# A causal softmax layer of a four-layer kernel: the order of the first transfers, and unread products on TensorE in the head

## The chip, the cores and the metric

The kernel runs on one core of a Trainium2 chip. The metric is the time of one execution on the device, in microseconds (us). Several executions are made, and their median is given.

## The reference

Four blocks are applied one after another to x of shape (8, 1024, 256), each as x + layernorm(block(layernorm(x))): causal softmax attention with 16 heads of 16, a linear layer, linear attention with a small feed-forward part, and a mixture of eight experts. The change touches only the part of the kernel that computes the first two, and there the softmax attention:

```python
qkv = x @ W_qkv + b_qkv
q, k, v = jnp.split(qkv, 3, axis=-1)          # 16 heads of 16
att = jnp.einsum('bhqd,bhkd->bhqk', q, k) * SCALE
att = jnp.where(causal, att, -jnp.inf)
att = jax.nn.softmax(att, axis=-1)
y = jnp.einsum('bhqk,bhkd->bhqd', att, v)
return y.transpose(0, 2, 1, 3).reshape(B, T, C) @ W_proj + b_proj
```

## The kernel before

`softmax_layer` works through the eight batches, one a turn. Five instruction streams (SyncE, TensorE, ScalarE, GpSimd, VectorE) are written out by hand and meet only at semaphores. Each stream has a part `before()`, the head, which prepares batch 0, and then `turn(b, ...)` for each batch.

**A turn** has 48 steps k: four head groups of four heads, twelve segments (`SEGS`) each. In a step TensorE does two pairs of score products (`scores`, K by Q, 50 rows of the array, two heads in the two halves of the array at once), two pairs of products for the row maxima (`maxima`, Q by K, 48 rows) of the segment 16 steps later (LM = 16), and the value products (`values`) of step k - 2. VectorE reduces the maxima products (`reduce`), with a mask added where a tile lies on the diagonal. ScalarE takes the exponentials of the scores. Maxima and scores share a ring R of three slots in PSUM, `psum_r`.

**Units** are further pieces of TensorE work, one after certain k by the table `UNIT_AT`, in a ring G of one slot, `psum_g`. Head units prepare the next batch: T1 (transposes of the normed x), QK (six products of 128x128x512 that make a half of Q or K for eight heads, in split precision), V. Tail units (END, YT, P, T2, F) finish the batch before. OUT and N belong to the batch itself: OUT transposes the attended values, and N transposes the maxima, which VectorE negates and splits (`minus`) and SyncE puts into `q_st` (`minus_max`, four transfers); the scores of the head group wait for them. Turn 0 has no tail units (`with_tail` is false). With them absent, steps 0 to 7, 9 and 10 of turn 0 have no unit but N 1 at 8; steps 28 to 31 have none either. `G.wait_free(pe, r, u)` waits until the unit before u has been evacuated.

**The head** runs T1, QK 0 to 3 and V 0 to 3. ScalarE copies each QK product to `parts` with its bias, GpSimd splits it in two. `stack(0, hg)` on SyncE then moves Q and K of head group hg from `parts` into `q_st` and `k_st` in twelve transfers of 128 KB; the head's first group waits for the splits of QK 0 to 3. TensorE's maxima of mk = 0 wait for all of stack(0, 0), those of mk = 12 for stack(0, 1). Maxima for mk = 0 to 15 follow, with QK 4 to 7 after mk = 4 to 7 and N 0 after mk = 12. Before ScalarE writes QK 4 into `parts` it waits for both stacks, which read that tile:

```python
if i % 4 == 0 and b + m > 0:
    for hg in (2 - 2 * m, 3 - 2 * m):
        act.wait_ge(stacked[hg], (b + m) * STACK)
```

`load_x(1, 0, GU_BEFORE)` is the load of batch 1 into `x_in`, 1 MB. It waits until the last T1 unit of batch 0 has been evacuated. VectorE first reads it at k = 1 of turn 0. All of SyncE's transfers are issued in program order, each after its own waits.

Of the kernel before, what the change touches and what calls it, by code (L numbers as in the profile page):

```python
# [15 lines left out]
P = 128  # L16
B, T, D = 8, 1024, 256
N = B * T
# [3 lines left out]
HALF = 512  # L22
# [100 lines left out]
def of_batch(view, b):  # L123
    return view[bass.ds(b, 1), :, :, :].rearrange("a p j d -> p (a j) d")
# [170 lines left out]
def softmax_layer(nc, ctx, ident, minus_half, spot, x_rows, W_qkv, b_qkv, W_proj, b_proj, weight,  # L295
# [13 lines left out]
    NSEG = len(SEGS)  # L309
# [7 lines left out]
    def sb(name, shape, dt=F32):  # L317
        return ctx.enter_context(nc.sbuf_tensor(name, shape, dt))
# [6 lines left out]
    psum_g = ctx.enter_context(nc.psum_tensor("a_general", [P, HALF], F32))  # L325
# [6 lines left out]
    w_qkv = {part: sb(f"w_qkv_{part}", [P, CD, 3 * D], F32R) for part in ("hi", "lo")}  # L332
# [167 lines left out]
    def kept(what, with_head, with_tail):  # L500
        if what[0] in TAIL_UNITS:
            return with_tail
        return with_head or not (what[0] in HEAD_UNITS or what == ("N", 4))
# [5 lines left out]
    def r_units(u0, with_head):  # L509
        units = {}  # L510
        for k in range(NK):
            for pair in range(2):
# [5 lines left out]
    H_SEQ = ([("T1", i) for i in range(4)] + [("QK", i) for i in range(4)] +  # L518
             [("V", i) for i in range(4)] + [("QK", i) for i in range(4, 8)] + [("N", 0)])
# [4 lines left out]
    GU_BEFORE = {what: i for i, what in enumerate(H_SEQ)}  # L524
# [8 lines left out]
    G = Ring(sem, "a_general", 1, PER_G)  # L533
# [40 lines left out]
    def of_sync(sp, prepare):  # L574
# [11 lines left out]
        def load_x(b, r, U):  # L586

            G.wait_evacuated(sp, r, U["T1", 3])
            sp.dma_start(x_in[:, :, :], of_batch(xv, b)).then_inc(x_loaded, 16)

        def stack(b, hg, used=None):

            if used is not None:
                sp.wait_ge(pv_done, used + PV0)
            if hg % 2 == 0:
                sp.wait_ge(split_done, 8 * b + 4 * (hg // 2) + 4)
            for qk, terms, st in ((0, QPART, q_st), (1, KPART, k_st)):
                for t, part in enumerate(terms):
                    for h2 in range(2):
                        to = 64 * h2 + DH0 * t  # L600
                        src = 64 * (hg % 2) + 32 * h2
                        sp.dma_start(
                            st[to:to + DH0, 2 * hg:2 * hg + 2, :].bitcast(F32),
                            parts[src:src + 32, qk, part, :].bitcast(F32)
                            ).then_inc(stacked[hg], 16)
# [22 lines left out]
        def turn(b, U, with_head, with_tail, more, prepare=None):  # L628
# [21 lines left out]
                sp.wait_ge(x2_stored, b * 16)  # L650
            sp.dma_start(x_res[:, :, :], of_batch(xv, b)).then_inc(res_loaded, 16)

        load_x(1, 0, GU_BEFORE)
        stack(0, 0)
        stack(0, 1)
        minus_max(0, 0, GU_BEFORE, 0)
        stack(0, 2)
# [22 lines left out]
    def of_tensor(pe, prepare):  # L680
        def four_turned(src, of, c):
            for j in range(4):
                last = nc.tensor.transpose(psum_g[:, j * P:(j + 1) * P], of(src, j, c),
                                           ident[:, :])
            return last

        def tile_of(half):
            return lambda src, j, c: src[:, half * 4 + j, c * P:(c + 1) * P]
# [10 lines left out]
        def two_tiles_split(i, lhs, rhs):  # L699
            for jj in range(2):  # L700
                j = 2 * i + jj
                terms = [(c, a, w) for c in range(CD) for a, w in PRODUCTS]
                for t, (c, a, w) in enumerate(terms):
                    last = nc.tensor.matmul(psum_g[:, jj * D:(jj + 1) * D],
                                            lhs[a][:, c, j * P:(j + 1) * P], rhs[w][:, c, :],
                                            start=(t == 0), stop=(t == len(terms) - 1))
            return last

        def unit(b, r, U, what):


            name, i = what
            u = U[what]
            if name == "T1":
                pe.wait_ge(head_norm, b * 4 + 2 * (i // CD) + 2)
            elif name == "T2":
                pe.wait_ge(tail_norm, b * 4 + 2 * (i // CD) + 2)
            elif name in ("OUT", "END"):
                v = i if name == "OUT" else 2 * HG - 1
                pe.wait_ge(attended, b * 2 * HG + v + 2)  # L720
            elif name == "N":
                pe.wait_ge(mx_ready, b * HG + i % HG + 1)
            G.wait_free(pe, r, u)
            if name == "T1":
                last = four_turned(x_in, tile_of(i // CD), i % CD)
            elif name == "T2":
                last = four_turned(att, tile_of(i // CD), i % CD)
            elif name == "YT":
                last = four_turned(y, tile_of(i // CD), i % CD)
            elif name in ("OUT", "END"):  # L730
                half = v % 2
                last = four_turned(oT, lambda src, j, c: src[:, half, j * P:(j + 1) * P], 0)
            elif name == "N":
                par = i % 2
                last = nc.tensor.matmul(psum_g[0:32, 0:P],
                                        mx[:, par, :, :, :].rearrange("p h r j -> p (h r j)"),
                                        ident[:, :], start=True, stop=True)
            elif name == "QK":
                m, qk, half = i // 4, i // 2 % 2, i % 2
                terms = [(c, a, x) for c in range(CD) for a, x in PRODUCTS]  # L740
                for t, (c, a, x) in enumerate(terms):
                    last = nc.tensor.matmul(psum_g[:, :],
                                            w_qkv[a][:, c, qk * D + m * P:qk * D + (m + 1) * P],
                                            xnT[x][:, c, half * HALF:(half + 1) * HALF],
                                            start=(t == 0), stop=(t == len(terms) - 1))
            elif name == "V":
                last = two_tiles_split(i, xnT, {part: w_qkv[part][:, :, 2 * D:3 * D] for part in w_qkv})
            elif name == "P":
                last = two_tiles(i, yT, w_proj)
            elif name == "F":  # L750
                last = two_tiles(i, yT, w_ffn)
            last.then_inc(G.full[0], 1)

        def maxima(b, r, U, mk, pair):
            hg, (j, k0, k1) = mk // NSEG % HG, PIECES[mk % NSEG]
            u, w = U["M", mk, pair], k1 - k0
            if mk % NSEG == 0 and pair == 0:
                pe.wait_ge(stacked[hg], (b + 1) * STACK)
            R.wait_free(pe, r, u)
            for h2 in range(2):  # L760
                rows = slice(64 * h2, 64 * h2 + KQ)
                last = nc.tensor.matmul(psum_r[:, R.slot(u), h2, 0:w],  # L762
                                        q_st[rows, 2 * hg + pair, j * P:(j + 1) * P],
                                        k_st[rows, 2 * hg + pair, k0:k1], start=True,
                                        stop=True)
            last.then_inc(R.full[R.slot(u)], 1)
# [35 lines left out]
        def batch_of(b, what):  # L802
            if what[0] in TAIL_UNITS:
                return b - 1
            return b + 1 if what[0] in HEAD_UNITS or what == ("N", 4) else b

        def turn(b, U, RU, with_head, with_tail, prepare=None):
            for k in range(NK):
                more = k + LM < NK or with_head
                scores(b, RU, k, 0)  # L810
                if more:
                    maxima(b + (k + LM) // NK, b, RU, k + LM, 0)
                if k > 1:
                    values(b, RU, k - 2)
                elif with_tail:
                    values(b - 1, RU_TURN, NK - 2 + k)
                scores(b, RU, k, 1)
                if more:
                    maxima(b + (k + LM) // NK, b, RU, k + LM, 1)
                if k in UNIT_AT and kept(UNIT_AT[k], with_head, with_tail):  # L820
                    unit(batch_of(b, UNIT_AT[k]), b, U, UNIT_AT[k])

        def before():
            for what in H_SEQ[0:12]:
                unit(0, 0, GU_BEFORE, what)
            for mk in range(LM):
                for pair in range(2):
                    maxima(0, 0, RU_BEFORE, mk, pair)
                if 4 <= mk < 8:
                    unit(0, 0, GU_BEFORE, ("QK", mk))  # L830
                if mk == NSEG:
                    unit(0, 0, GU_BEFORE, ("N", 0))

        turns(turn, before, prepare)

        def last_values():
# [2106 lines left out]
```

## Time and profile before

| what | value |
|---|---|
| median of three runs | 4213.46 us (4207.55 to 4227.06) |
| the profiled execution, its own time | 4220.28 us |
| its span | 4218.5 us |
| its mean granted TensorE clock | 0.963 |
| TensorE busy | 3896.9 us, 92% of the span |
| VectorE busy | 2709.6 us, 64% |
| head of the softmax layer | 0 to 103.6 us, where k = 0 of turn 0 begins |
| k = 0 to 15 | 103.6 to 165.5 us in turn 0, 261.5 to 315.7 us in turn 1 |

Times in the rows count from the start of the span. In a row of windows stand the window, its length, then the busy us (and instructions begun) of PE (TensorE's products), PEld (its weight loads), DVE (VectorE), ACT (ScalarE) and POOL (GpSimd), then the granted clock, the busy share of the 16 transfer engines, and GB/s. In a row of waits stand who waited for whom, us in total, times, and the longest. In a timeline, a row is the start, the length until the last of the merged instructions ended, the engine, the line of the kernel, the operation with what it writes and reads, and in brackets the idle time before it and what ended it. The granted clock is a share of the full 2.4 GHz: 1.00 is 2.4 GHz, 0.50 is 1.2 GHz, and a value between the two is a stretch with some of each.

### The profile page before, as it was taken

Reading aid. Unit: us, or ns where it says so; the run is one execution under the profiler, and the core shown is the slowest. Engines: PE = TensorE matmul, PEld = TensorE weight load, DVE = VectorE, ACT = ScalarE, POOL = GpSimd, SP = SyncE. Lnnn points to the kernel's source line nnn. Section 1 sums busy time; section 2 is a strip of 40 time slices with the busy share of each in tenths; the row PEclk is TensorE's granted clock in tenths of the full one; section 3 lists DMA queues with packets and bytes.
Section 4 is the critical chain, followed back from the end, with each engine's and each line's share of the span. In section 5 each row is a group of like instructions: output and inputs, shape, how many; then the busy total and the mean of one; then the engine's idle time right before and its main releaser. Section 6 shows DMA issues by size and latency. Waiting matters only on the chain. (4 is left out here: it accounts for less than half of the span.)

```text
span 4218.5 us, 74666 instructions
## 1 busy us (share of the span) xinstructions
PE 3896.9 (92%) x28676; PEld 3028.7 (72%) x28676; DVE 2709.6 (64%) x7827; ACT 2115.5 (50%) x3994; POOL 1162.1 (28%) x1097
## 2 busy tenths in 40 slices
PE   4999999999999899999999999999999699999992
PEld 2444444444445788888888888888888599999992
DVE  5788988888885566555565665555565555555555
ACT  1566666666666555555455554454454333333323
POOL 3234344343332211111112111111111133333334
PEclk8799999999988999999999999999999799999996
DMA  3543543544441100000000000000001133333336
GB/s 70 98 87 50 114 92 57 97 92 67 77 100 53 36 26 21 21 21 23 18 22 22 22 20 17 16 20 11 18 20 34 52 65 71 70 65 69 70 60 191
DMA packets 176195, 227.06 MB, mean 54 GB/s; under 512 B 27276, under 2 KB 152299, under 8 KB 175840
## 3 DMA queue, kind: packets, MB, share of 16 engines
q1 hardware_dynamic: 147808, 185.86, 19.3%
q0 software_dynamic: 26736, 31.70, 4.9%
q8 instruction: 228, 3.74, 0.4%
q10 hardware_dynamic: 1296, 4.72, 0.3%
q14 instruction: 127, 1.04, 0.1%
HBM read 90.63 MB, written 87.05 MB: 42 GB/s over the span
## 5 line engine op out<-in xcount | busy, mean ns | idle before, releaser
L882 ACT ACTIVATE probs<-a_scores 128x1024 f32<-128x1024 f32 (+3 forms) x768 | 615.5, 811 | 342.7 <-PE a_scores L776 337.3
L1036 DVE CUSTOM_DVE_ANT_0 a_scores<-a_scores,mask 128x384 f32<-128x384 f32 (+3 forms) x1024 | 480.3, 513 | 107.9 <-PE a_scores L762 102.4
L776 PEld LDWEIGHTS a_scores<-q_st,k_st 50*128 50x128 f32 x1536 | 149.6, 192 | 358.9 <-issue 206.6
L275 POOL TENSOR_TENSOR l_ln_rstd<-l_ln_ve,minus_half 128x4 f32<-128x4 f32 x80 | 81.9, 1023 | 1047.2 <-DVE l_ln_ve L248 1046.8
L1844 ACT ACTIVATE l_o<-l_num,l_den 128x64 f32<-128x64 f32 x960 | 222.0, 319 | 291.4 <-DVE l_den L2330 286.6
L776 PE MATMUL a_scores<-q_st,k_st 50*128 50x512 f32 (+3 forms) x1536 | 350.6, 454 | 11.6 <-DVE mx L1036 5.4
L762 PE MATMUL a_scores<-k_st,q_st 48*128 48x512 f32 (+3 forms) x1536 | 307.6, 398 | 50.6 <-ACT probs L882 23.0
L796 PE MATMUL a_out<-probs,v_aug 128*32 128x512 f32 (+3 forms) x3072 | 348.6, 528 | 3.5 <-POOL probs L963 3.3
L1039 DVE TENSOR_REDUCE mx<-a_scores 128x2 f32<-128x1024 f32 x256 | 309.8, 1221 | 59.3 <-PE a_scores L762 58.3
L963 POOL TENSOR_SCALAR_AFFINE_SELECT probs<-probs 128x512 f32<-128x512 f32 x256 | 164.2, 642 | 524.0 <-ACT probs L882 515.0
L2647 PE MATMUL e_out<-e_weights_hi,e_hT_hi 128*128 128x256 f32 x1088 | 303.8, 279 | 0.0
L2647 PE MATMUL e_out<-e_weights_hi,e_hT_lo 128*128 128x256 f32 x1088 | 303.8, 279 | 0.0
L2647 PE MATMUL e_out<-e_weights_lo,e_hT_hi 128*128 128x256 f32 x1088 | 303.7, 279 | 0.0
L2694 ACT ACTIVATE e_to_split<-e_hidden,e_b 128x384 f32<-128x384 f32 (+1 forms) x320 | 200.0, 625 | 196.9 <-PE e_hidden L2632 196.5
L1753 PE MATMUL l_num<-l_v,l_scores_kept 128*128 128x65 f32 x2048 | 285.1, 262 | 0.0
L1753 PEld LDWEIGHTS l_num<-l_v,l_scores_kept 128*128 128x128 f32 x2048 | 270.0, 192 | 0.0
L1858 ACT ACTIVATE l_o<-l_general 128x512 f32<-128x512 f32 x256 | 152.6, 596 | 219.4 <-PE l_general L1602 200.3
L2716 POOL DMA_INDIRECT expert_sums_scratch<-e_y,e_number x136 | 222.6, 1637 | 69.7 <-issue 37.4
L762 PEld LDWEIGHTS a_scores<-k_st,q_st 48*128 48x128 f32 x1536 | 155.0, 198 | 115.0 <-ACT probs L882 80.2
L2231 DVE TENSOR_TENSOR l_a<-l_general,l_a 128x512 f32<-128x512 f32 x64 | 44.3, 692 | 299.2 <-PE l_general L1561 160.8
L2632 PE MATMUL e_hidden<-e_rT_hi,e_weights_hi 128*128 128x384 f32 (+1 forms) x640 | 233.8, 365 | 0.0
L1748 PE MATMUL l_num<-l_state,l_qT 128*128 128x130 f32 x1024 | 231.0, 307 | 0.0
(278 smaller groups left out, 10560.3 us busy)
## 6 DMA issues: line engine op xcount, KB each, us to landing
q_st<-parts SPq DMA_DIRECT2D x192, 128.0 KB, 4.5
k_st<-parts SPq DMA_DIRECT2D x192, 128.0 KB, 6.8
expert_rows_scratch<-empty_row SPq DMA_DIRECT2D x34, 520.0 KB, 9.6
l_x<-x_scratch SPq DMA_DIRECT2D x32, 512.0 KB, 3.8
e_weights<-in_L_ffn_W_dram SPq DMA_DIRECT2D x16, 1024.0 KB, 6.9
e_rows<-expert_rows_scratch SPq DMA_DIRECT2D x24, 390.0 KB, 3.2
e_rows<-expert_rows_scratch SPq DMA_DIRECT2D x16, 520.0 KB, 3.8
x_in<-in_L_attn_x_dram SPq DMA_DIRECT2D x8, 1024.0 KB, 5.5
```

What stands on the lines that cost most here:

```text
L762: last = nc.tensor.matmul(psum_r[:, R.slot(u), h2, 0:w], q_st[rows, 2 * hg + pair, j * P:(j + 1) * P], k_st[rows, 2 * hg + pair, k0:k1], s ...
L776: last = nc.tensor.matmul(psum_r[:, R.slot(u), h2, 0:w], k_st[rows, 2 * hg + pair, i * P:(i + 1) * P], q_st[rows, 2 * hg + pair, q0:q0 + w ...
L796: last = nc.tensor.matmul(psum_o[32 * h4:32 * h4 + 32, q0 - half * HALF:HALF], v_aug[:, i, h * DV0:h * DV0 + 32], probs[:, k % 3, h4, 0:w] ...
L882: nc.scalar.activation(probs[:, k % 3, 2 * pair:2 * pair + 2, 0:w], psum_r[:, R.slot(u), :, 0:w], ACT.Exp).then_inc(R.evacuated[R.slot(u)], 1)
L1036: last = nc.vector.tensor_tensor_reduce(s, s, mask[:, HALF - w:HALF], 1.0, LEAST, ALU.add, ALU.max, out[:, h2, :])
L1039: last = nc.vector.tensor_reduce(out.rearrange("p h a -> p (h a)"), psum_r[:, R.slot(u), :, 0:w], AX.X, ALU.max)
L1748: nc.tensor.matmul(psum_n[:, NUM.slot(n), p2 * 2 * DV:(p2 + 1) * 2 * DV], qT[:, p, j * P:(j + 1) * P], state[:, p, :], start=True, stop=Fa ...
L1753: last = nc.tensor.matmul(psum_n[:, NUM.slot(n), h4 * DV:(h4 + 1) * DV], scores[:, d % 2, h2, p % 4, :], v_aug[:, j, 4 * g4 + h4, :], star ...
L1844: last = nc.scalar.activation(o[:, j % 2, head:head + DH1], psum_n[:, NUM.slot(n), h * DV:h * DV + DH1], ACT.Copy, scale=den[:, n % 2, 1, ...
L2632: last = nc.tensor.matmul(psum_h[:, HU.slot(u), 0:n * P], w1[a][:, e2, c, m * P:(m + 1) * P], rT[b][:, q % 2, c, 0:n * P], start=(k == 0), ...
L2647: last = nc.tensor.matmul(psum_y[:, s, (j - 2 * s) * D:(j - 2 * s + 1) * D], hT[a][:, q % 2, m, j * P:(j + 1) * P], w2[b][:, e2, m, :], st ...
L2716: nc.gpsimd.indirect_dma_start(out=sums_dram, out_offset=bass.IndirectOffsetOnAxis(ap=number[:, q % RING, j:j + 1], axis=0), in_=y[:, q % ...
```

## The change

It has two parts. On SyncE, stack(0, 0) is issued ahead of the load of batch 1; the other orders stay. On TensorE, a new function `full_rows` issues products of 128x128x512 whose result in `psum_g` nobody reads: sixteen after the V units; two after each pair of maxima for mk = 0 to 3, 8 to 11 and 13 to 15 (sixteen, sixteen and twelve); and in turn 0 three after each of k = 1, 2, 4 and 5 (twelve). All wait for the slot of G to be free: those of mk = 8 to 11 for the evacuation of QK 7, those of mk = 13 to 15 and of turn 0 for that of N 0.

```diff
+        stack(0, 0)
         load_x(1, 0, GU_BEFORE)
-        stack(0, 0)
         stack(0, 1)
         minus_max(0, 0, GU_BEFORE, 0)
         stack(0, 2)
...
                 if k in UNIT_AT and kept(UNIT_AT[k], with_head, with_tail):
                     unit(batch_of(b, UNIT_AT[k]), b, U, UNIT_AT[k])
+                if not with_tail and k in FIRST_FULL:
+                    full_rows(0, U["N", 1], 3)
+
+        FIRST_FULL = (1, 2, 4, 5)
+
+        def full_rows(r, u, count):
+
+            G.wait_free(pe, r, u)
+            for n in range(count):
+                nc.tensor.matmul(psum_g[:, :], w_qkv["hi"][:, 0, 0:P], w_qkv["hi"][:, 0, 0:HALF],
+                                 start=True, stop=True)
 
         def before():
             for what in H_SEQ[0:12]:
                 unit(0, 0, GU_BEFORE, what)
+            full_rows(0, GU_BEFORE["QK", 4], 16)
             for mk in range(LM):
                 for pair in range(2):
                     maxima(0, 0, RU_BEFORE, mk, pair)
+                    if mk < 4:
+                        full_rows(0, GU_BEFORE["QK", 4], 2)
+                    elif 8 <= mk < NSEG:
+                        full_rows(0, GU_BEFORE["N", 0], 2)
+                    elif NSEG < mk:
+                        full_rows(0, len(H_SEQ), 2)
```

## Rows read from the trace of the kernel before

**Rows 1.** The page: busy time (us, share of the span, instructions) and clock by slice.
```profile
PE 3896.9 (92%) x28676; PEld 3028.7 (72%) x28676; DVE 2709.6 (64%) x7827; ACT 2115.5 (50%) x3994; POOL 1162.1 (28%) x1097
...
PEclk8799999999988999999999999999999799999996
```

**Rows 2.** Windows of 1 us at the four changes of the clock.
```profile
62.00:63.00 1.00, 0.00 (x0) 0.00 (x0) 0.00 (x0) 0.00 (x0) 0.37 (x1) 0.67 1.04 135
79.00:80.00 1.00, 0.84 (x6) 0.49 (x5) 0.17 (x1) 0.69 (x1) 0.00 (x1) 0.79 0.00 0
89.00:90.00 1.00, 0.59 (x2) 0.19 (x2) 1.00 (x2) 0.00 (x0) 0.70 (x1) 0.83 0.00 0
157.00:158.00 1.00, 1.00 (x8) 0.00 (x0) 0.99 (x5) 0.00 (x0) 0.00 (x0) 0.54 1.09 335
```

**Rows 3.** TensorE's timeline in the head.
```profile
44.87 0.40 PE L742 MATMUL a_general<-xnT_hi,w_qkv_lo 128*128 128x512 f32 x1
...
45.81 0.39 PE L742 MATMUL a_general<-xnT_lo,w_qkv_hi 128*128 128x512 f32 x1
...
67.61 1.54 PE L762 MATMUL a_scores<-k_st,q_st 48*128 48x512 f32 x6 [9.09 <-DMA k_st<-parts]
...
76.18 0.79 PE L742 MATMUL a_general<-xnT_hi,w_qkv_hi 128*128 128x512 f32 x1
76.77 0.63 PE L742 MATMUL a_general<-xnT_hi,w_qkv_lo 128*128 128x512 f32 x1
...
78.48 0.63 PE L742 MATMUL a_general<-xnT_lo,w_qkv_hi 128*128 128x512 f32 x1
```

**Rows 4.** Windows by stage, columns as in rows 2.
```profile
86.30:89.70 3.40, 1.91 (x11) 0.86 (x10) 2.72 (x3) 0.69 (x1) 3.28 (x3) 0.99 0.00 0
103.60:157.90 54.30, 51.10 (x234) 20.39 (x234) 37.84 (x118) 27.50 (x39) 9.21 (x13) 0.50 0.51 86
103.60:165.50 61.90, 58.61 (x296) 24.22 (x296) 44.06 (x137) 32.94 (x48) 10.48 (x15) 0.56 0.53 104
261.50:315.70 54.20, 51.52 (x368) 25.21 (x366) 49.68 (x155) 37.21 (x56) 15.29 (x20) 0.97 0.77 160
202.30:205.70 3.40, 2.85 (x24) 1.21 (x20) 3.17 (x4) 2.79 (x4) 1.71 (x2) 1.00 1.05 127
205.70:219.40 13.70, 13.01 (x50) 4.12 (x50) 8.35 (x18) 6.02 (x7) 0.00 (x0) 0.50 0.39 50
```

**Rows 5.** VectorE's timeline in the head.
```profile
86.98 6.88 DVE L1039 TENSOR_REDUCE mx<-a_scores 128x2 f32<-128x1024 f32 x6 [1.36 <-PE a_scores L762]
```

**Rows 6.** VectorE's waits, 103.6 to 157.9 us.
```profile
DVE a_scores L1036 <- PE a_scores L762: 10.3, 8, 1.7
DVE mx L1039 <- PE a_scores L762: 4.7, 6, 1.8
```

**Rows 7.** Timeline of SyncE's DMA queue: issues.
```profile
38.38 0.39 SPq L589 DMA_DIRECT2D x_in<-in_L_attn_x_dram  x1
51.84 3.83 SPq L602 DMA_DIRECT2D q_st<-parts  x6
...
59.53 4.93 SPq L602 DMA_DIRECT2D q_st<-parts  x6
...
99.84 1.17 SPq L612 DMA_DIRECT2D q_st<-nm_hi  x2
```

**Rows 8.** Windows around the load and around the stacks.
```profile
39.00:44.00 5.00, 3.97 (x12) 2.37 (x10) 0.00 (x0) 0.90 (x2) 1.79 (x2) 1.00 0.65 210
53.00:77.00 24.00, 10.35 (x51) 6.92 (x51) 10.47 (x37) 0.00 (x0) 3.03 (x3) 0.69 1.01 132
```

**Rows 9.** Line 602, 67.5 to 68.5 us: the last two issues of stack(0, 1).
```profile
L602 SPq DMA_DIRECT2D k_st<-parts x2: 592/592/592, 67.0 to 67.7; - x2
...
DMA to landing us min/median/max: 10.2/10.2/10.2
```

**Rows 10.** ScalarE's timeline in the head.
```profile
79.23 0.69 ACT L859 ACTIVATE parts<-a_general,bias_qk 128x512 f32<-128x512 f32 x1 [29.88 <-PE a_general L742]
```

## The prediction

> **What bounds the kernel now.** I began with the page. TensorE is busy for 92% of the span, and the clock row shows where it is slow: 8 and 7 tenths in the first two slices, hardly below 9 for the rest [rows 1]. So the change works where the clock is poor, in the first 210 us. That is 5% of the kernel, which already limits what it can be worth.
>
> Next I read the granted clock in windows of one microsecond [rows 2]. It falls from 2.4 GHz (1.00) to 1.2 GHz (0.50) at 62.3, rises at 79.4, falls at 89.7 and rises only at 157.9. (A mean of 0.67 over 62 to 63 says that the fall came a third of the way in; the others are read alike.) The TensorE timeline says what the engine had done [rows 3]. Ahead of the first fall it had stood idle since 58.5 (67.61 less 9.09), and it idled on until 67.61, when the first stack of Q and K had landed. Ahead of the second it issued small products of 48 rows at VectorE's pace, busy 1.91 of 3.4 us [rows 4]. The slow stretch that counts is the last, 68 us long.
>
> What ends last in it? From 89.7 to 103.6 VectorE never pauses: its reductions follow one another (six take 6.88 us, first row of [rows 5]), so a faster TensorE gains nothing there. From 103.6, where turn 0 begins, TensorE is busy 51.1 of 54.3 us at 1.2 GHz and VectorE only 37.84 [rows 4]. The waits of VectorE say the same: 10.3 + 4.7 us for TensorE's maxima products [rows 6]. There TensorE bounds the kernel and its clock matters.
>
> **The load moved behind the first stack.** The name suggests that the stack gets in earlier. It does not. SyncE issued the load at 38.38 and then stood waiting for the split; stack(0, 0) was issued at 51.84 in either order [rows 7]. What the load needs of the transfer engines is 0.65 x 5.0 = 3.25 us [rows 8]. They are full from 53 to 77 (share 1.01) with the 24 transfers of the two stacks. In the new order the load enters this full stretch behind the twelve transfers of stack(0, 0), at 59.5, and the twelve of stack(0, 1) come 3.25 us later. SyncE's extra issue of 0.39 us lies below that, since it runs ahead of the engines.
>
> Who waits for stack(0, 1)? ScalarE does: `take` for ("QK", 4) waits for stacked[0] and stacked[1] before it overwrites `parts`. The last transfer of stack(0, 1) lands at 67.7 + 10.2 = 77.9 [rows 9], and ScalarE's work started at 79.23, for TensorE's product [rows 10]. Now the landing is at 77.9 + 3.25 = 81.2, so the wait costs **+2.0 us**. Behind it stand ("QK", 5) to 7 on the single slot of psum_g, the maxima from mk = 6 on, and the whole head: nothing gives it back, because VectorE has only the sums of mk = 5 left. TensorE idles here for some 3 us, a stand of the kind that preceded the first fall, so I add **+0.5** for ("QK", 5) starting slow (0 if the clock holds; 6 x (0.43 - 0.23) = 1.2 at most). If the load instead mixed into stack(0, 0), the first maxima would start up to 3.25 us late, 70.9 instead of 67.61; the 8.6 us until ("QK", 4) and its 2.6 us (76.18 to 78.91, slow) then end at about 82, 0.9 beyond the 81.2. The load itself is wanted at k = 1 of turn 0, at about 110: some 40 us of cover.
>
> The Trainium skill (DMA: Bandwidth & Descriptors, Queues, rings and completion order) says that descriptors on an engine are taken in ring order, and that a semaphore's increment lands after the earlier writes of that engine. By that the load cannot hold up stack(0, 0), and the price would be the 2.0; no transfer in the trace before shows a load between the stacks.
>
> **The unread products.** One of 128x128x512 takes 0.235 us at 2.4 GHz (four from 44.87 to 45.81) and 0.43 us at 1.2 GHz (four from 76.77 to 78.48) [rows 3].
> - Sixteen ahead of the stack: they begin within 1 us of 58.5, once VectorE has evacuated V 3, and take 16 x 0.235 = 3.8 us, inside 9.09 us of idle. Cost 0. They leave over 4 us of idle behind, so I count the first maxima as slow, as before.
> - Sixteen among mk = 0 to 3: at 1.2 GHz 6.9 us more on TensorE. With the maxima (2.1 us, at 0.43 per pair of 512 columns and less in proportion) that is 9.0 us, plus 0.9 for mk = 4 and 2.6 for ("QK", 4): 67.6 + 12.5 = 80.1, below the 81.2 of the stack. Cost 0, by that cover alone; without it +0.9 against 79.23.
> - Sixteen among mk = 8 to 11: per pair 0.22 + 0.47 = 0.69 us fast, below VectorE's 1.15 (6.88/6): cost 0. Slow: 0.43 + 0.86 = 1.29, so 8 x 0.14 = 1.1. Their wait for ("QK", 7) ends about 1 us after its product, while VectorE is in its first 1.15 us reduction.
> - Twelve among mk = 13 to 15: they wait for `minus`, which VectorE does between its reductions; it has one pair ready then. Fast: 6 x 0.47 + 0.6 = 3.4 us, below the 3.8 us from the issue of `nm_hi` at 99.84 [rows 7] to the first scores at 103.6: cost 0. Slow: 6 x 0.86 + 1.3 = 6.4, so +2.6.
> - Twelve in turn 0 (k = 1, 2, 4, 5): 2.8 us of TensorE fast, hidden if VectorE bounds; slow 12 x 0.43 = 5.2, all on the path.
>
> **What they buy.** They stand in for the tail's units, absent in turn 0. Turn 1 does the same k (0 to 15) with those units at a clock of 0.97 in 54.2 us, VectorE busy 49.68, or 92%; turn 0 takes 61.9 us with VectorE at 44.06 [rows 4]. If the clock holds, turn 0 takes at most 54.2 (-7.7), and at VectorE's 92% 44.06/0.92 = 48 (-14). TensorE would then have 51.1/2 + 7.5 + 2.8 = 36 us of work, far from the bound, so I take a value near the second, 50: **-11.9 us**. Does it hold? In turn 1 the clock holds through most stretches of this kind, k with no unit among them; it fell at 205.7 in k = 29, a place with no unit and narrow value products, busy 2.85 of 3.4 us [rows 4]. k = 4 and 5 are of that kind and get products; k = 6, 7, 9 and 10 get none, but have value products of 512 columns. I think it holds, without certainty.
>
> The Trainium skill (TensorE: Matmul & The Clock Gate, HAM oscillation) describes a kernel whose clock falls in each wait for a transfer and whose next products start slow. By that sixteen products that end well before the stack lands are wasted, and the later ones must do the work; the fall at 62.3 agrees.
>
> Sum: -11.9 + 2.0 + 0.5 = -9.4. The profiled execution took 4220.28 (span 4218.5); that gives 4211. It was 6.8 us above the median of 4213.46, so I forecast **4204 us**, 0.22% faster. About 0.5%, 21 us, is what a measurement of this kernel can tell from no change: the three runs themselves lie 19.5 us apart.
>
> **The rivals.**
> - *The slow clock stays* (0.20). The place is mk = 12 to k = 1: TensorE waits for `minus`, then works at VectorE's pace with no value products, and if the clock falls there the additions don't raise it, as nothing raised it from 89.7 to 157.9. Then there is no gain, and +2.0 + 1.1 + 2.6 + 5.2 = +10.9: 4224 us, slower than before. For it: TensorE 94% busy at 1.2 GHz did not bring it back. Against: full products did at 79.4. It decides as soon as the clock is at 0.50 when k = 0 begins.
> - *It holds to k = 6 to 10 and falls then* (0.18). Eight of the sixteen steps, half of the 11.9, are won: -6 + 2.5 = -3.5, 4210 us. For it speak the steps without unit or product.
> - *More than that* (0.10). The later slow stretch, 205.7 to 219.4, goes too (13.7 to 8.35/0.92 = 9.1, -4.6) and the stack's wait is not felt: -16.5, 4197 us.
> - The forecast has 0.52.
>
> **How the numbers follow.** The term of 7.7 to 14 gives 4202 to 4209 for the forecast alone; runs scatter by several us around it. From 4197 to 4224, with that scatter, a range of **4192 to 4222** leaves out about half of the first rival and a little below. No case reaches 21 us either way, so only scatter can: faster 0.09, same 0.87, slower 0.04.
>
> **What would show it.** TensorE's idle before the first maxima at 4 to 5 us instead of 9.1, with those maxima still at about 67.6; ScalarE's `parts` for ("QK", 4) ended by the stack at about 81; a granted clock of 1.00 from about 90 to beyond 150; k = 0 at about 106; the load of batch 2 issued 9 to 10 us earlier. I am wrong if the clock is 0.50 at k = 0, or if the stack lands before TensorE's product.

## The result, and the profile after

The change makes the kernel slower: the ratio of its times to those of the kernel before is 1.0035, with a 95% interval of 1.0025 to 1.0046. Its median is 4231.85 us (20 runs) beside 4216.94 us for 20 runs of the kernel before, 14.9 us more. I had forecast 4204 us and 0.22% faster, with a range that ended at 4222. The profiled execution of the changed kernel has a span of 4234.9 us.

The page of the changed kernel answers to [rows 1]. The first two slices have a faster clock (9 and 8 tenths where they had 8 and 7), the third a slower one (8 where it had 9), and the span is longer:

```profile
PE 3932.7 (93%) x28748; PEld 3048.0 (72%) x28748; DVE 2712.6 (64%) x7827; ACT 2114.4 (50%) x3994; POOL 1161.0 (27%) x1097
...
PEclk9889999999999999999999999999999799999996
```

TensorE's timeline of the changed kernel in the head answers to [rows 3]. L831 is the unread product, in groups:

```profile
59.30 3.92 PE L831 MATMUL a_general<-w_qkv_hi 128*128 128x512 f32 x16 [0.79 <-DVE v_new L1100]
66.61 0.80 PE L762 MATMUL a_scores<-k_st,q_st 48*128 48x512 f32 x2 [3.38 <-DMA k_st<-parts]
67.34 1.22 PE L831 MATMUL a_general<-w_qkv_hi 128*128 128x512 f32 x2
68.49 0.79 PE L762 MATMUL a_scores<-k_st,q_st 48*128 48x512 f32 x2
...
80.32 1.22 PE L762 MATMUL a_scores<-k_st,q_st 48*128 48x512 f32 x4
81.47 0.79 PE L742 MATMUL a_general<-xnT_hi,w_qkv_hi 128*128 128x512 f32 x1
...
105.75 0.82 PE L831 MATMUL a_general<-w_qkv_hi 128*128 128x512 f32 x2 [2.36 <-DVE nm_lo L1076]
106.50 0.69 PE L762 MATMUL a_scores<-k_st,q_st 48*128 48x384 f32 x2
...
113.54 1.22 PE L831 MATMUL a_general<-w_qkv_hi 128*128 128x512 f32 x2
114.69 0.79 PE L776 MATMUL a_scores<-q_st,k_st 50*128 50x512 f32 x2
```

Three things are to be seen. The sixteen products in the wait do what was expected: 9.09 us of idle became 3.38, and the first stack even came 1 us earlier. From 66.61 until QK 4 is done TensorE never idles; the eight pairs of mk = 0 to 3 take it until 80.32, and QK 4 begins at 81.47 instead of 76.18. And after `minus` the twelve last products stand ahead of the first scores: TensorE gets to k = 0 only at 114.69, without waiting for anything but its own work. Before, it was there at 103.6. The head is 11.1 us longer.

ScalarE's first `parts` of the head's second half answers to [rows 10]. It was taken at 84.52 for TensorE's product, not at 81.2 for the stack:

```profile
84.52 0.69 ACT L877 ACTIVATE parts<-a_general,bias_qk 128x512 f32<-128x512 f32 x1 [35.16 <-PE a_general L742]
```

SyncE's issue of `nm_hi` answers to the last row of [rows 7]. From it to k = 0 it is 9.0 us, where it was 3.8:

```profile
105.72 1.17 SPq L612 DMA_DIRECT2D q_st<-nm_hi  x2
```

The windows of the changed kernel answer to [rows 4]: the stretch from the first maxima to that product, the one after `minus`, k = 0 to 15 of turn 0, and two of the clock's changes (falls at 65.3 and 106.2):

```profile
66.60:84.50 17.90, 17.89 (x44) 8.77 (x46) 10.41 (x34) 0.00 (x0) 0.00 (x0) 0.50 0.73 120
...
105.70:114.70 9.00, 8.95 (x24) 4.23 (x24) 5.25 (x24) 0.00 (x0) 0.00 (x0) 0.53 0.63 97
114.70:168.30 53.60, 50.70 (x309) 22.29 (x308) 42.96 (x129) 33.25 (x48) 10.42 (x15) 0.79 0.53 104
65.00:66.00 1.00, 0.00 (x0) 0.00 (x0) 0.00 (x0) 0.00 (x0) 0.00 (x0) 0.63 1.06 187
...
106.00:107.00 1.00, 1.00 (x4) 0.33 (x3) 0.74 (x4) 0.00 (x0) 0.00 (x0) 0.61 0.02 6
```

In the first, TensorE is busy for 17.89 of 17.9 us and VectorE for 10.41: TensorE bounds a stretch in which VectorE did before. In the last of the stages turn 0 does get faster, 53.6 us where [rows 4] have 61.9, with a clock of 0.79. Together that is only +2.8 us, and the other turns of this trace are longer too. So two questions went to the chip: which part of the head costs what, and how much of the gain in turn 0 is the products' own.

### The profile page after: what moved, and what is told of

It is laid out like the page before. It is cut to its first block and busy times, and to the rows that moved or that the text cites. A ratio compares the mean times of both kernels' runs of the same rounds, so it can differ in the third digit from the quotient of the medians.

```text
span 4234.9 us, 74810 instructions
## 1 busy us (share of the span) xinstructions
PE 3932.7 (93%) x28748; PEld 3048.0 (72%) x28748; DVE 2712.6 (64%) x7827; ACT 2114.4 (50%) x3994; POOL 1161.0 (27%) x1097
## 5 line engine op out<-in xcount | busy, mean ns | idle before, releaser
L2734 POOL DMA_INDIRECT expert_sums_scratch<-e_y,e_number x136 | 221.6, 1629 | 69.7 <-issue 37.3
L2249 DVE TENSOR_TENSOR l_a<-l_general,l_a 128x512 f32<-128x512 f32 x64 | 44.3, 692 | 299.2 <-PE l_general L1579 160.8
L2650 PE MATMUL e_hidden<-e_rT_hi,e_weights_lo 128*128 128x384 f32 (+1 forms) x640 | 230.7, 360 | 0.0
```

Source lines behind the costliest of these rows:

```text
L2650: last = nc.tensor.matmul(psum_h[:, HU.slot(u), 0:n * P], w1[a][:, e2, c, m * P:(m + 1) * P], rT[b][:, q % 2, c, 0:n * P], start=(k == 0), ...
L2734: nc.gpsimd.indirect_dma_start(out=sums_dram, out_offset=bass.IndirectOffsetOnAxis(ap=number[:, q % RING, j:j + 1], axis=0), in_=y[:, q % ...
```

## The experiments

Two theories were set against each other. P: the slowdown comes from the head, where the unread products put TensorE time on the path and the moved load a wait. C: any shift of the head moves the slow stretches of the clock in later turns, and most of the time is lost there.

The experiments were read by one ruler, since what precedes it varies from execution to execution: the time from SyncE's issue of the first stack (the first `q_st<-parts`) to three events in the same trace. They are ScalarE's take of QK 4, the first scores of k = 0, and the issue of the third `nm_hi`, after k = 20; the last column counts from k = 0 to that issue. Times in the table are us. Of the kernels, `full_rows` and its calls are as in the changed kernel unless a diff says otherwise.

| kernel | take of QK 4 | k = 0 | k = 0 to 20 |
|---|---|---|---|
| before, three traces | 27.4, 27.3, 27.4 | 51.8, 51.7, 51.8 | 76.8, 69.7, 76.8 |
| changed, three traces | 32.7, 32.6, 32.3 | 62.8, 62.8, 62.7 | 68.6, 68.7, 73.0 |
| order_only | 30.0 | 56.6 | 69.9 |
| no_first | 30.0 | 62.2 | 66.9 |
| no_last | 30.9 | 55.8 | 64.8 |
| turn_only | 27.3 | 51.7 | 73.2 |
| no_turn | 32.3 | 62.6 | 69.9 |
| gap_only | 27.5 | 51.9 | 69.8 |
| middle_turn | 29.2 | 54.0 | 81.3 |
| old_order | 33.3 | 63.6 | 72.0 |
| first_only | 33.6 | 58.0 | 76.5 |
| first_grouped, grouped_b | 26.8, 27.4 | 51.3, 51.7 | 75.0, 71.2 |
| grouped_mid | 28.2 | 53.0 | 76.5 |

**order_only: the order alone.**

```diff
+        stack(0, 0)
         load_x(1, 0, GU_BEFORE)
-        stack(0, 0)
```

> The order of stack and load alone, no unread product. Theory P (the slowdown of 15 us is TensorE time that the unread products put on the path of the head, plus the load's wait): +0 to +2 us against the kernel before, since the last transfer of stack(0, 1) lands near 80.5 instead of 77.9 and ScalarE needed it at 79.2. Theory C (any shift of the head moves the slow stretches of the clock in later turns, and most of the 15 us comes from there): up to some +10 us here too, though the head is hardly longer.

The ratio is 1.0008 (0.9992 to 1.0024). The head shows what that hides. ScalarE's timeline in this kernel:

```profile
85.63 0.69 ACT L859 ACTIVATE parts<-a_general,bias_qk 128x512 f32<-128x512 f32 x1 [32.46 <-DMA k_st<-parts]
89.33 0.69 ACT L859 ACTIVATE parts<-a_general,bias_qk 128x512 f32<-128x512 f32 x1 [3.02 <-PE a_general L742]
92.75 0.69 ACT L859 ACTIVATE parts<-a_general,bias_qk 128x512 f32<-128x512 f32 x1 [2.73 <-PE a_general L742]
```

Now it waits for the stack, as the prediction had it: 30.0 us behind the issue instead of 27.4. And the next two come 3.7 and 3.4 us apart instead of 2.4: TensorE stood idle for 4.08 us meanwhile, and QK 5 and most of QK 6 ran at 1.2 GHz. The first row of QK 5 in TensorE's timeline:

```profile
86.37 0.79 PE L742 MATMUL a_general<-xnT_hi,w_qkv_hi 128*128 128x512 f32 x1 [4.08 <-ACT parts L859]
```

The order costs 4.8 us by k = 0, twice what I had charged, and more than the 0 to 2 us that I expected of this run. The time does not tell it from zero.

**no_first: without the products of mk = 0 to 3.**

```diff
-                    if mk < 4:
-                        full_rows(0, GU_BEFORE["QK", 4], 2)
-                    elif 8 <= mk < NSEG:
+                    if 8 <= mk < NSEG:
```

> The changed kernel without the sixteen unread products among mk = 0 to 3. Theory P: QK 4 is evacuated near 80.5 to 81 instead of 84.5, 4 us of the 15 come back, so about +11 us against the kernel before. Theory C: the time stays near +15 us, or moves without relation to the 4 us.

The ratio is 1.0017 (1.0004 to 1.0030), +7 us. QK 4 is taken at 30.0, again for the stack, but k = 0 is only 0.6 us earlier than in the changed kernel: the wait behind the load and the slow products that follow it take the place of the sixteen. I had expected 4 us back.

**no_last: without the products of mk = 13 to 15.**

```diff
-                    elif NSEG < mk:
-                        full_rows(0, len(H_SEQ), 2)
```

> The changed kernel without the twelve unread products among mk = 13 to 15. Theory P: k = 0 begins 4 us behind the issue of nm_hi instead of 9, so 5 us come back and the time is about +10 us against the kernel before; if these twelve are what raises the clock by k = 3, the clock stays slow in turn 0 and its 8 us of gain are lost, about +18 us. Theory C: near +15 us.

The ratio is 1.0020 (1.0003 to 1.0037), +8 us. TensorE's timeline shows the first scores waiting for the transfer of `nm_lo` again, as in the kernel before, instead of for products that nobody reads:

```profile
107.90 0.47 PE L762 MATMUL a_scores<-k_st,q_st 48*128 48x128 f32 x2 [0.29 <-DVE mx L1052]
108.92 0.80 PE L776 MATMUL a_scores<-q_st,k_st 50*128 50x512 f32 x2 [0.55 <-DMA q_st<-nm_lo]
```

The head is 7 us shorter than the changed one (55.8). Of these, 1.8 are there already when QK 4 is taken (30.9 beside 32.7), ahead of the place of the edit; the twelve themselves account for the other 5.2. Turn 0 keeps its gain (64.8), so they buy nothing here.

**turn_only and no_turn: the twelve of turn 0 alone, and all but them.** The first is the kernel before with the call in `turn` and `full_rows`; the second has

```diff
-        FIRST_FULL = (1, 2, 4, 5)
+        FIRST_FULL = ()
```

> The kernel before with only the twelve unread products of turn 0 (k = 1, 2, 4, 5). Theory P: if they raise the clock in turn 0 as in the changed kernel, -8 us; if the clock stays slow they cost 12 x 0.43 us and the switches, +6 to +7 us. Theory C: no relation to the clock of turn 0; up to +10 us.

> The changed kernel without the twelve unread products of turn 0. Theory P: the head's 11 us remain and the gain of turn 0 (turn_only: -4.6 us) is missing, so about +19 us against the kernel before, 1.0045. If the products of turn 0 only cost, it is faster than the changed kernel, about +10 us.

turn_only: 0.9989 (0.9974 to 1.0005), inconclusive, -4.6 us if anything. no_turn: 1.0041 (1.0023 to 1.0060), +17 us. Against the changed kernel's 1.0035 and 1.0031 the twelve are worth nothing that these intervals can tell. One trace suggests why. In turn_only the clock was slow when they came, three of them took 1.65 us, and k = 0 to 20 took 73.2 us, more than the 69.7 of the kernel before in its second trace.

**gap_only: the sixteen in the wait alone**, in the old order:

```diff
+            full_rows(0, GU_BEFORE["QK", 4], 16)
             for mk in range(LM):
```

> The kernel before with the sixteen unread products in the wait for the first stack, and nothing else changed, the order of the load neither. Theory P: they end 4 us before the stack lands and are free; the maxima may start at 2.4 GHz, where VectorE bounds them anyway, so 0 within 3 us. Theory C: a few us either way, because the clock enters the head otherwise.

The ratio is 1.0004 (0.9994 to 1.0014). The sixteen are free here, but not always; see middle_turn.

**before_b and before_c, after_b and after_c: both kernels again, unchanged.**

> The kernel before once more, unchanged, for a second trace. Theory P: from the first stack's issue to k = 0 it takes the same 51.8 us as in the first trace and in turn_only, whatever the clock. What the clock does in turn 0 and later differs from execution to execution: if 76.8 us from k = 0 to the third nm_hi of turn 0 (k = 20) was an unlucky value, it is nearer to the 70 us of order_only here. Time: ratio 1.000 within the interval.

> The changed kernel once more, unchanged. Theory P: about 62.8 us from the first stack's issue to k = 0 again (it was 62.8 and, without the first sixteen, 62.2), ratio 1.0035 again within 0.002. Slow stretches of the clock in later turns at other places and of another total than the 113 us of the first trace; theory C wants them as many and as long as there, and more than in before_b.

> The kernel before, a third trace: k = 0 at 51.8 us behind the stack's issue; from there to the third nm_hi of turn 0 between 69 and 77 us; slow stretches of the clock in turns 1 to 6 anywhere between 7 and 60 us in total.

> The changed kernel, a third trace: k = 0 at 62.8 us; from there to the third nm_hi of turn 0 between 68 and 75 us. If the 4 us of the slowdown that the head and turn 0 leave open come from later turns, the slow stretches there are 55 to 92 us in total again; if it is chance, they are anywhere from 7 us on.

before_b: 1.0007 (0.9990 to 1.0023). after_b: 1.0031 (1.0020 to 1.0043), so the slowdown is real. The two others are one execution each (4224.07 and 4238.8 us). The window of k = 0 to 20 in the first trace of the kernel before:

```profile
103.60:180.40 76.80, 72.50 (x378) 30.48 (x378) 56.20 (x161) 42.59 (x58) 18.08 (x22) 0.65 0.47 97
```

The same steps in before_b:

```profile
107.40:177.10 69.70, 64.11 (x378) 27.39 (x378) 55.62 (x160) 42.54 (x58) 18.03 (x22) 0.78 0.53 107
```

In the changed kernel's first trace:

```profile
114.70:183.40 68.70, 64.74 (x391) 28.55 (x390) 55.29 (x153) 42.97 (x58) 18.03 (x22) 0.84 0.46 97
```

In after_c:

```profile
118.40:191.40 73.00, 68.00 (x391) 29.75 (x390) 55.29 (x153) 42.87 (x58) 18.08 (x22) 0.79 0.44 90
```

The same kernel takes 76.8 us with a clock of 0.65 and 69.7 with 0.78. The changed one takes 68.6 or 73.0. The prediction had been made on the 76.8.

The two values go with how the execution began. SyncE's issue of the first stack in before_b, the changed kernel's first trace and after_c, in this order, beside the 51.84 of [rows 7]:

```profile
55.68 3.83 SPq L602 DMA_DIRECT2D q_st<-parts  x6
...
51.85 3.83 SPq L602 DMA_DIRECT2D q_st<-parts  x6
...
55.69 3.83 SPq L602 DMA_DIRECT2D q_st<-parts  x6
```

Of the ten traces without products in turn 0, the five that issue it at 51.8 to 51.9 us take 75.0 to 76.8 us for k = 0 to 20, and the five that issue it at 54.4 to 55.7 take 69.7 to 71.2. With the change it is the other way round: 68.6 and 68.7 us after an issue at 51.8, 73.0 after one at 55.7. So turn 0 gains 8 us in executions of the first kind and loses 3 in those of the second, where only one trace of each kernel stands. No run forced either kind, and the timed executions do not tell which they were.

**old_order: the changed kernel with the load ahead again.**

```diff
+        load_x(1, 0, GU_BEFORE)
         stack(0, 0)
-        load_x(1, 0, GU_BEFORE)
```

> The changed kernel with the old order of load and stack. Theory P: in the changed kernel TensorE's unread products hide the wait for the second stack (QK 4 was evacuated for TensorE's product, not for the stack), so undoing the order gives nothing back: the first stack lands 1 us later and k = 0 comes 63 to 64 us behind the stack's issue, ratio 1.0035. The rival, by which the load's place costs its 4.8 us of order_only here too: k = 0 at 58 us, ratio 1.002.

The ratio is 1.0041 (1.0025 to 1.0057), with k = 0 at 63.6, within the 63 to 64 of theory P. The costs do not add. While the sixteen products hold TensorE, the wait behind the load lies under them.

**first_only and first_grouped: what makes the sixteen dear.** Both are the kernel before with the products of mk = 0 to 3 only. The second has four behind each mk instead of two behind each pair:

```diff
-                    if mk < 4:
-                        full_rows(0, GU_BEFORE["QK", 4], 2)
+                    if mk < 4 and pair == 1:
+                        full_rows(0, GU_BEFORE["QK", 4], 4)
```

> The kernel before with only the sixteen unread products among mk = 0 to 3, two behind each pair. ScalarE takes QK 4 at 27.4 us behind the first stack's issue in the kernel before and at 32.7 in the changed one. Theory P: 33 to 34 here, since nothing but these products moves it (the old order lets the stack land 1 us later).

> The same sixteen products, but four behind the second pair of each mk: four changes between half-array and full products instead of eight. If the changes cost (0.3 us each way at 1.2 GHz, as the starts 0.73 and 1.15 us apart instead of 0.43 and 0.86 suggest), QK 4 is taken 2.4 us earlier than in first_only, at about 31. If each product simply takes longer than 0.43 us, there is no difference.

> The kernel before with only the sixteen products among mk = 0 to 3, four behind each mk, timed. Theory P: 51 to 52 us from the stack's issue to k = 0 (51.3 in the first look), clock at 2.4 GHz within 6 us of the first maxima, and a time within 0.1% of the kernel before: the head is bound by VectorE and turn 0 goes its own way. Rival: each earlier rise of the clock is worth something in turn 0, then -3 to -5 us.

QK 4 is taken at 33.6 and 26.8 us, a difference of 6.8 where I expected 2.4. TensorE's timeline in first_only:

```profile
67.58 0.80 PE L762 MATMUL a_scores<-k_st,q_st 48*128 48x512 f32 x2 [9.04 <-DMA k_st<-parts]
68.30 1.22 PE L831 MATMUL a_general<-w_qkv_hi 128*128 128x512 f32 x2
69.45 0.79 PE L762 MATMUL a_scores<-k_st,q_st 48*128 48x512 f32 x2
...
80.13 1.22 PE L831 MATMUL a_general<-w_qkv_hi 128*128 128x512 f32 x2
81.28 1.22 PE L762 MATMUL a_scores<-k_st,q_st 48*128 48x512 f32 x4
```

In first_grouped:

```profile
67.64 1.22 PE L762 MATMUL a_scores<-k_st,q_st 48*128 48x512 f32 x4 [9.10 <-DMA k_st<-parts]
68.79 2.07 PE L831 MATMUL a_general<-w_qkv_hi 128*128 128x512 f32 x4
70.79 1.01 PE L762 MATMUL a_scores<-k_st,q_st 48*128 48x384 f32 x4
...
75.13 1.20 PE L831 MATMUL a_general<-w_qkv_hi 128*128 128x512 f32 x4
76.26 0.73 PE L762 MATMUL a_scores<-k_st,q_st 48*128 48x512 f32 x4
```

Read the starts. In first_only a pair of maxima and two products take 1.87 us (67.58 to 69.45), 0.72 + 1.15, where I had counted 0.43 + 0.86: each change from half-array to full products costs 0.3 us at 1.2 GHz, and each change back as much. In first_grouped four maxima products and four unread ones take 3.15 us, 1.15 + 2.00, so the changes are half as many (four maxima products alone would need 0.86). That accounts for 2.4 us. The rest is the clock: with four in a row it rose near 72.5, and four products soon took 1.20 us; with two in a row it stayed at 1.2 GHz to the end of the sixteen, though TensorE was busy throughout. All seven traces with these products in twos agree; in the three with fours the clock rose among them, 5 to 8 us after the first maxima. grouped_b, timed, is 1.0010 (0.9991 to 1.0029): the cost in the head is gone, and no gain shows. Its QK 4 at 27.4 and k = 0 at 51.7 are those of the kernel before.

**middle_turn and grouped_mid: only what seemed free.** middle_turn has the old order, the sixteen in the wait, those of mk = 8 to 11 and those of turn 0; grouped_mid is first_grouped with those of mk = 8 to 11.

> The old order of the load, with the unread products that cost no time on the path: sixteen ahead of the stack, sixteen among mk = 8 to 11, twelve in turn 0; none among mk = 0 to 3 and mk = 13 to 15. Theory P: from the first stack's issue to k = 0 it takes 52 us as in the kernel before (62.8 in the changed one); those of mk = 8 to 11 keep or bring the clock, so that from k = 0 to the third nm_hi of turn 0 it takes 65 to 67 us (64.8 in no_last) against 70; in all -3 to -5 us against the kernel before, ratio 0.999. Theory C: no relation, up to +10 us.

> The same with the sixteen products among mk = 8 to 11, two behind each pair, which cost nothing in the changed kernel's trace at 2.4 GHz. Theory P: k = 0 at 51 to 53 us behind the stack's issue and the clock at 2.4 GHz until N 0; then it depends on mk = 13 to 15, where nothing is added. Time 0 to -4 us against the kernel before. If these products fall into a slow stretch, up to +2 us in the head.

middle_turn is slower, 1.0016 (1.0002 to 1.0030); theory P is wrong about it. grouped_mid is 1.0004 (0.9986 to 1.0022). The sixteen in the wait, in middle_turn's timeline:

```profile
68.07 5.59 PE L831 MATMUL a_general<-w_qkv_hi 128*128 128x512 f32 x16 [0.78 <-DVE v_new L1096]
```

And the window of its k = 0 to 20:

```profile
109.70:191.00 81.30, 76.93 (x390) 33.55 (x390) 56.39 (x160) 43.06 (x58) 18.07 (x22) 0.67 0.46 92
```

In this execution the V products before had run at half pace, so the sixteen began 12.4 us behind the stack's issue instead of 7.45 (59.30 less 51.85 in the changed kernel), ran slow at first, and held the maxima up by 2.2 us. In turn 0 the clock stayed low, and the twelve were paid in full: 81.3 us, the longest of all. The same twelve products that go with 65 us in one execution (no_last) go with 81 in this. No version beat the kernel before by more than its interval.

Taken together, the timed ratios rise with the head. The four kernels with k = 0 by 53.0 us (turn_only, gap_only, grouped_b, grouped_mid) have 0.9989 to 1.0010. Those with it at 62.6 or later (the changed one twice, no_turn, old_order) have 1.0031 to 1.0041. no_first, with 62.2 and 1.0017, fits worst.

## Why the prediction was wrong

**The step that failed first is "Cost 0" for the sixteen among mk = 0 to 3 and the cost of the twelve among mk = 13 to 15.** The pairs of mk = 0 to 3 with their products were to take 9.0 us at 1.2 GHz and took 13.7 (66.61 to 80.32), because sixteen changes of 0.3 us each (two for each of eight pairs) were left out. The trace before hinted at such a change: in [rows 3] the first product of QK 4 starts 0.59 us ahead of the second, the others 0.43. So TensorE became the bound, the 81.2 of the stack no longer covered it, and QK 4 was taken at 84.5. I had named this cover as the only one.

**The twelve among mk = 13 to 15** were counted at nothing for a fast clock and at 2.6 us for a slow one. The clock fell at 106.2, as they began, and with the changes they and the maxima between them took 8.9 us (105.75 to 114.69). Their price is the time from the issue of `nm_hi` to k = 0: 9.0 us instead of 3.8, and 3.9 in no_last. The 11 us of head are thus 5.3 up to the take of QK 4, 0.6 from there to `nm_hi`, and 5.2 for these twelve.

**The load** was sized at +2.0 and +0.5, and it costs 4.8 us of head when alone (order_only): 2.6 for the wait and 2.2 for the slow products behind it. That the stack would not be earlier by the whole load was right. It came 1 us earlier: its last transfer landed 7.7 us after its issue instead of 8.7, the ones ahead of it as before. That it no longer shares the engines with the next stack's transfers is my reading, which no run isolates. In the changed kernel the load costs nothing (old_order), because the unread products lie over its wait. The three terms together were to give +2.5 and gave 10.9 to 11.1, in each of three traces.

The clause of the Trainium skill on ring order (DMA: Bandwidth & Descriptors, Queues, rings and completion order) agrees with the traces here: the load behind the first stack did not delay it, 66.61 beside 67.61. So does its account of a clock that falls in a wait for a transfer (TensorE: Matmul & The Clock Gate, HAM oscillation): the sixteen products ahead of the stack did not keep the clock, it fell at 65.3 and the maxima began slow. In no_last, no_turn and old_order it fell within 2 us after the first of them.

**The second failed step is the -11.9 of turn 0.** Its mechanism, that TensorE bounds a slow turn 0, was right; the 61.9 us it started from belonged to one kind of execution, and even there 8.3 were won instead of 11.9 (53.6 us). Over k = 0 to 20 the kernel before needs 76.8, 69.7 and 76.8 us, the changed one 68.6, 68.7 and 73.0: 4.3 us less on average, 8 less or 3 more by the kind. Over all traces, the ten without products in turn 0 average 73.2 us (69.7 to 76.8) and the eight with them 71.1 (64.8 to 81.3). The clock did not hold in turn 0 either: it was slow at its beginning and from 147.2 to 160.8, in steps with value products of fewer columns among them. The sign that I had named for being wrong came true: the clock was at 0.50 when k = 0 began. The rival "the slow clock stays" had the right sign and, at +10.9, nearly the size; its place was half right, since the clock fell at mk = 13, yet came back at k = 2. Its size was luck: it counted no gain in turn 0 and +5.2 for the products there, and left out the changes that the head paid for.

**Sum.** +11.0 in the head and -2 to -4 in turn 0 give +7 to +9 us. Measured were +14.9 (10.5 to 19.4) and, in after_b, +13, so 4 to 8 us stay open. In the traces the open time lies behind turn 0's k = 20: from there to the end of the span the three traces of the kernel before take 4038.0, 4036.1 and 4041.9 us, those of the changed one 4051.6, 4049.2 and 4045.7, 10 us more on average and without overlap; 7 of the 10 fall into the softmax turns, 3 behind them. This is where theory C looks for the time, and for this part nothing here refutes it. Against it stand old_order, with the same unread products and 4033.5 us, and no_turn, with 4039.1; for it, no_first and no_last, with 4049.5 and 4046.1. Slow stretches of the clock in turns 1 to 6 add up to 7, 7 and 58 us in the three traces of the kernel before and to 92, 55 and 27 in those of the changed one; the kernels between lie at 7 to 65 with no order by what they contain. They are part of the scatter and do not give the 10 us by themselves: before_c, with 58, takes less than after_c, with 27. Whether the changed kernel draws more of them on average, three traces cannot tell. The clock row of [rows 1], too, shows slices of 8, 8 and 7 tenths far behind the first two, where I had read "hardly below 9".

## What to carry to other kernels

Products issued only to keep a clock up are work on an in-order engine: whatever is queued behind them waits, and they are dearest exactly when the clock is low. Price them with the change of shape between neighbours, at the slow clock, against the slack of the engine that bounds the stretch. And when a gain is read from the clock of one trace, take a second trace of the same kernel first, and compare traces that began alike; here the same stage took 69.7 and 76.8 us.

## What was not expected of the hardware

- A change between products of 48 rows in the two halves of the array and products of 128 rows cost TensorE about 0.3 us at 1.2 GHz, each way, and 0.2 at 2.4 GHz (a pair and two products every 1.10 us at mk = 8 to 11, where 0.69 was counted). It does not depend on the columns: at 1.2 GHz the product behind a pair of 512, 384, 256 and 128 columns starts 0.72, 0.62, 0.51 and 0.40 us after the pair, each time 0.3 more than the columns take.
- TensorE was busy for 17.89 of 17.9 us, with full products in twos between the pairs of maxima, and the granted clock stayed at 0.50. With the same products in fours it rose 5 us after the first maxima in first_grouped, 6 in grouped_b and 8 in grouped_mid.
- The granted clock in the records can be wrong before its first change. In middle_turn it reads 1.00 from 60 to 65 us, and V products start 0.21 us apart there, where the kernel before has 0.12; in order_only it reads 1.00 from 76 to 82 us, and the products of QK 4 start 0.43 us apart. The row of middle_turn's windows:

```profile
60.00:65.00 5.00, 3.57 (x15) 3.27 (x16) 1.28 (x2) 0.00 (x0) 0.00 (x0) 1.00 1.07 129
```

And two rows of its timeline in that window:

```profile
61.24 0.42 PE L704 MATMUL a_general<-w_qkv_lo,xnT_hi 128*128 128x256 f32 x1
61.46 0.41 PE L704 MATMUL a_general<-w_qkv_hi,xnT_hi 128*128 128x256 f32 x1
```
